# Issuing two 64-row merge products of a block inverse in turn on two quarters of TensorE

## The chip, the cores and the metric

The kernel runs on one core of a Trainium2 chip. The metric is the device time of one execution in microseconds (us), the median of several runs. The engines are named as the profile names them: PE (TensorE, matrix products), PEld (its weight loads), DVE (VectorE), ACT (ScalarE), POOL (GpSimd) and SP (SyncE, which issues most DMAs).

## The reference

One layer of a small language model over an input of 2 sequences of 2048 tokens with 128 channels. The first half is a gated delta rule with 8 heads of 128 by 128 state; the second half is a mixture of 8 experts with top-2 routing. What matters here is the recurrence of the first half:

```python
def step(S, inp):
    q_t, k_t, v_t, beta_t, alpha_t = inp
    S = S * alpha_t[..., None, None]
    kv = jnp.einsum('bhk,bhkv->bhv', k_t, S)
    S = S + jnp.einsum('bhk,bhv->bhkv', k_t, (v_t - kv) * beta_t[..., None])
    o_t = jnp.einsum('bhk,bhkv->bhv', q_t, S)
    return (S, o_t)
```

Taken over a chunk of 128 tokens, these steps become matrix products, and one of the factors is the inverse of a unit triangular 128 by 128 matrix for each head.

## The kernel before

**Tiling.** The 4096 tokens are 32 chunks of 128, worked on in 16 groups of two chunks (`GC = 2`, chunk 0 and chunk 1 of the group). A round of the program finishes group g (the inverse's merges, the solution, the state update, the output) while it prepares group g + 1 (projections, convolution, the matrix to be inverted, and the inverses of its diagonal blocks on DVE). After the 16 groups comes the mixture of experts, which the change does not touch.

**Order.** Every engine runs its own instructions in the order of one list written out by hand, `ORDER` (lines 248 to 264), read once for each round. An entry names a step and its arguments; each engine issues its part of a step where the entry stands, so an entry's place sets the order of each engine's queue, and semaphores tie the engines together. In the last round nothing is prepared.

**The inverse.** DVE inverts the 32 by 32 diagonal blocks (step `inv`, lines 1029 to 1062). They go out to memory and come back (steps `to`, `tp`, `ti`, `tj`) into the tile `T64` (printed as `T` in the profile), and DVE transposes them into `R` (step `rdiag.0` for blocks 1 and 3, `rdiag.1` for blocks 0 and 2, line 1187). Then, for each chunk c, four steps `m.c.hop` on PE with a copy `me.c.hop` on ACT behind each build the rest of the inverse (function `merge`, lines 1460 to 1501):

- hop 0 and hop 1 make the off-diagonal 32 by 32 blocks. Their products stand on 32-row and 32-column parts of PE, two or three streams in turn (lines 1469 and 1470, then 1480 to 1482).
- hop 2 is the last but one product: `Nm[0:64]` against `T64[0:64]`, 8 heads, one 64 by 64 product each, from partitions 0 to 63 to partitions 64 to 127 (line 1490). It waits for `r32_sb` (the copy behind hop 1, lines 808 to 810).
- hop 3 is the last product: `Y64[64:128]` against `R[64:128]`, 8 heads, from partitions 64 to 127 to partitions 0 to 63 (line 1500). It waits for `rdiag.1` and for `y64_sb` (the copy behind hop 2, line 813). The copy behind it, line 817, sets `R_ready`, which the step `u` waits for (line 1602).

A 32-bit product is recorded as two passes, so 8 heads give 16 instructions. Chunk 0's hops 0 and 2 write the bank `ob0` and hops 1 and 3 write `ob1`; chunk 1's write `kx0` and `kx1`. Each hop begins with one or two `carry` products (line 1386), small 16-bit products on all rows whose result is overwritten.

**The steps around it.** `proj` is a projection (lines 1551 to 1553); `taps`, `first`, `last` are the convolution behind it on ACT (766), DVE (1144, 1147) and POOL (639). `kk` forms key products (line 1539, released to DVE's `nm`, line 1163), `ks` the key-state product (1597, then `rhs` on ACT, 822), `u` the solution (1606), `sp` scales the state on POOL (651), `scan` is a decay scan on DVE (1155). The matrices that `nm` makes are written to memory (`no`) and read back (`bi`) before DVE can start the next inverse (line 1042).

The stretch of the order in question runs: `m.1.2 ... proj.6 rdiag.1 me.1.2 m.0.2 ... proj.7 ... kk.0.0 ... m.1.3 ks.0.1 taps.7 me.0.2 proj.8 rhs.0.0 first.7 proj.9 ... me.1.3 m.0.3 ... kk.0.1 ... kk.1.0 u.0.0`.

Of the kernel before, what the change touches and what calls it, by code (L numbers as in the profile page):

```python
# [6 lines left out]
def preln_delta_moe_kernel(nc, x_in, qkv_t, z_t, ab_t, conv_w, dt_bias, a_log, norm_w, out_t,  # L7
# [6 lines left out]
    H = ab_t.shape[1] // 2  # L14
# [31 lines left out]
    with ctx:  # L46
# [18 lines left out]
        wab_lo = sb("wab_lo", [128, 2 * H], F16)  # L65
# [5 lines left out]
        taps = sb("taps", [128, NT, TAPS])  # L71
# [20 lines left out]
        Nm, AT = part(1, 0), part(1, 1)  # L92
        kd = part(2, 0)
        squares, spare = part(2, 1)[:, 0], part(2, 1)[:, 1]
        R, zg = part(3, 0), part(3, 1)
# [5 lines left out]
        T64 = sb("T64", [128, GC, H, 2 * BLK])  # L101
# [7 lines left out]
        rhs = sb("rhs", [128, H, C])  # L109
# [57 lines left out]
        merge_banks = [ob, kx]  # L167
# [58 lines left out]
        def rsqrt_step(s, v, y, t):  # L226
# [21 lines left out]
        ORDER = """  # L248
            v.0.0 diag.0 proj.0 proj.1 v.0.1 taps.0 first.0 proj.2 taps.1 first.1 rdiag.0 proj.3 taps.2 m.1.0 first.2 taps.3
            m.0.0 al.0 proj.4 me.1.0 aq.0 me.0.0 m.1.1 first.3 scan.0 m.0.1 last.0 al.1 xl.0 taps.4 last.1 me.1.1 first.4  # L250
            ka.0 proj.5 last.2 ac.0 ks.0.0 m.1.2 diag.1 taps.5 first.5 me.0.1 proj.6 rdiag.1 me.1.2 m.0.2 last.3 taps.6
            proj.7 last.4 kk.0.0 first.6 m.1.3 ks.0.1 taps.7 me.0.2 proj.8 rhs.0.0 first.7 proj.9 last.5 last.6 me.1.3 m.0.3
            nm.0.0 rhs.0.1 last.7 taps.8 sp.0 kk.0.1 scan.1 nm.0.1 first.8 last.8 me.0.3 kk.1.0 u.0.0 taps.9 kk.1.1 ue.0.0
            sm proj.10 taps.10 sd.0.0 u.0.1 ue.0.1 nm.1.0 nm.1.1 first.9 st.0.0 proj.11 taps.11 last.9 o.0.0 first.10 sq.0.0
            first.11 sd.0.1 ka.1 proj.12 proj.13 no.0 no.1 bi last.10 taps.12 last.11 ktr.0.0 taps.13 o.0.1 st.0.1 g.0.0
            v.1.0 scale.0 first.12 first.13 sq.0.1 ks.1.0 proj.14 kd.0.0 inv.0 rhs.1.0 aq.1 sp.1 proj.15 v.1.1 ks.1.1
            taps.14 taps.15 kq.0.0 inv.1 inv.2 u.1.0 rhs.1.1 u.1.1 g.0.1 inv.3 inv.4 inv.5 first.14 last.12 ue.1.0 ue.1.1
            inv.6 o.1.0 s2 o.1.1 inv.7 at.0.0 inv.8 inv.9 sd.1.0 sq.1.0 inv.10 inv.11 sq.1.1 ac.1 ktr.0.1 first.15 last.13
            inv.12 kd.0.1 last.14 ktr.1.0 last.15 rms.0 scale.1 kd.1.0 sd.1.1 rms.1 gn.0.0 kq.0.1 inv.13 gt.0.0 at.0.1
# [11 lines left out]
        def chunks(b, c):  # L271

            return (b + 1) * GC + c + 1

        def rounds(b):

            return b + 2
# [1103 lines left out]
        def _(pe):  # L1381
            mm, tr = nc.tensor.matmul, nc.tensor.transpose

            def carry(o, w=wab_hi):

                mm(o, w[:, :], w[:, :], start=True, stop=True)
# [44 lines left out]
            def bank_free(use, g, a, r=None):  # L1431

                uses = BANK_USES[bank_of(*use)]
                k = uses.index(use)
                waited = False
                for back in range(1, len(uses) + 1):
                    step, *arg = uses[k - back]
                    early, late = step in PREPARES, step in ROUTES
                    if k >= back:
                        b = a if early else r if late else None if isinstance(g, int) and g == NG else g  # L1440
                        sure = True
                    elif g is None:
                        return
                    elif late:
                        b = None if r is None or isinstance(r, int) and r == 0 else r - 1
                        sure = isinstance(r, int)
                    else:
                        b = g if early else g - 1
                        sure = early or isinstance(g, int) and g > 0
                    if b is None or waited and not early and not late:  # L1450
                        continue
                    if early and isinstance(b, int) and b >= NG:
                        continue
                    for taken, n in released(step, b, *arg):
                        pe.wait_ge(taken, n)
                    if sure:
                        return
                    waited = waited or not late

            def merge(g, a, r, c, hop):  # L1460

                y_bank, r_bank = merge_banks[c]
                if hop == 0:
                    pe.wait_ge(t_in, g * (16 * NB) + 16 * NB)
                    bank_free(("m", c, 0), g, a, r)
                    carry(y_bank[0:2 * H, 0:2 * H])
                    py = y_bank[:, 0:H * BLK].rearrange("p (h c) -> p h c", h=H)
                    for h in range(H):
                        mm(py[32:64, h], Nm[0:32, c, h, 32:64], T64[0:32, c, h, 0:32], start=True, stop=True)
                        ins = mm(py[96:128, h], Nm[64:96, c, h, 96:128], T32[64:96, c, h, :], start=True, stop=True)  # L1470
                    ins.then_inc(y32_mm[c], 1)
                elif hop == 1:
                    pe.wait_ge(rdiag, chunks(g, 0))
                    bank_free(("m", c, 1), g, a, r)
                    carry(r_bank[96:96 + 2 * H, 0:2 * H])
                    pe.wait_ge(y32_sb[c], rounds(g))
                    carry(r_bank[96:96 + 2 * H, 0:2 * H], wab_lo)
                    pr = r_bank[:, 0:H * BLK].rearrange("p (h c) -> p h c", h=H)
                    for h in range(H):
                        mm(pr[0:32, h], Y32[c][32:64, h, :], R[32:64, c, h, 32:64], start=True, stop=True)  # L1480
                        mm(pr[32:64, h], R[32:64, c, h, 32:64], Y32[c][32:64, h, :], start=True, stop=True)
                        ins = mm(pr[64:96, h], Y32[c][96:128, h, :], R[96:128, c, h, 96:128], start=True, stop=True)
                    ins.then_inc(r32_mm[c], 1)
                elif hop == 2:
                    pe.wait_ge(r32_sb[c], rounds(g))
                    bank_free(("m", c, 2), g, a, r)
                    carry(y_bank[0:2 * H, 0:2 * H])
                    py = y_bank[64:128, :].rearrange("p (h c) -> p h c", h=H)
                    for h in range(H):
                        ins = mm(py[:, h], Nm[0:64, c, h, 64:128], T64[0:64, c, h, :], start=True, stop=True)  # L1490
                    ins.then_inc(y64_mm[c], 1)
                else:
                    pe.wait_ge(rdiag, chunks(g, 1))
                    bank_free(("m", c, 3), g, a, r)
                    carry(r_bank[96:96 + 2 * H, 0:2 * H])
                    pe.wait_ge(y64_sb[c], rounds(g))
                    carry(r_bank[96:96 + 2 * H, 0:2 * H], wab_lo)
                    pr = r_bank[0:64, :].rearrange("p (h c) -> p h c", h=H)
                    for h in range(H):
                        ins = mm(pr[:, h], Y64[c][64:128, h, :], R[64:128, c, h, 64:128], start=True, stop=True)  # L1500
                    ins.then_inc(r64_mm[c], 1)

            def route(step, r, g, a):

# [22 lines left out]
            def stages(g, a, par):  # L1527
# [48 lines left out]
                def finish(step, arg):  # L1576

                    if step == "m":
                        merge(g, a, r, *arg)
                    elif step == "v":  # L1580

                        c, u = arg
# [186 lines left out]
```

## Time and profile before

| | us |
|---|---|
| median of 3 runs (lowest, highest) | 1470.88 (1468.65, 1473.63) |
| the profiled execution's own time | 1456.88 |
| its span, first to last instruction | 1454.8 |
| PE busy in it | 1207.4 |
| DVE busy in it | 1158.9 |
| ACT busy in it | 823.5 |
| POOL busy in it | 728.8 |

The profiled execution is 14.0 us shorter than the median of the runs; 2.1 us of its time lie outside the span. Matrix products on PE overlap, so the distance between the starts of two of them, not the length of one, says how fast PE gets through them. PE's granted clock has two levels in this trace, 2.4 GHz (shown as 1.00) and 1.2 GHz (0.50); its mean is 0.923.

### The profile page before, as it was taken

How to read it: one execution, taken by the hardware profiler on the slowest of the kernel's cores; microseconds unless marked ns; L12 is line 12 of the kernel's file. 1: busy time of each engine (PE TensorE's matmuls, PEld its weight loads, DVE VectorE, ACT ScalarE, POOL GpSimd, SP SyncE). 2: the span in 40 equal slices, each digit the busy share in tenths (PEclk: the TensorE clock that was granted, in tenths of full speed). 3: DMA queues.
4: the chain of work that ended last, by engine and by line, in shares of the span. 5: the costliest groups of instructions: out<-in, count | busy, mean ns of one | idle time of the engine just before them, and what ended most of it. 6: DMA issues, size and time to landing. Idle time of an engine off the chain costs nothing.

```text
span 1454.8 us, 33709 instructions
## 1 busy us (share of the span) xinstructions
PE 1207.4 (83%) x11978; PEld 985.3 (68%) x11978; DVE 1158.9 (80%) x2567; ACT 823.5 (57%) x2497; POOL 728.8 (50%) x601
## 2 busy tenths in 40 slices
PE   0356999999898989898989898989999896389980
PEld 0234868787787878786878686868777775267760
DVE  6878888888888788979788888888888853677774
ACT  1243666566656656575657666666565654255552
POOL 3143645546373737373737465555646341154544
PEclk9986989899999989999989998999999898699996
DMA  6031221213131303131222221221212152322214
GB/s 199 4 91 30 68 66 37 74 37 76 36 82 36 86 27 91 31 92 30 81 42 69 43 68 45 66 74 38 74 37 76 35 147 69 98 61 65 65 46 173
DMA packets 163174, 97.07 MB, mean 67 GB/s; under 512 B 115623, under 2 KB 148269, under 8 KB 161988
## 3 DMA queue, kind: packets, MB, share of 16 engines
q1 hardware_dynamic: 124932, 82.25, 20.8%
q10 hardware_dynamic: 33536, 4.20, 2.0%
q0 software_dynamic: 4544, 8.47, 1.8%
q8 instruction: 100, 1.64, 0.5%
q14 instruction: 62, 0.51, 0.1%
HBM read 73.31 MB, written 24.61 MB: 67 GB/s over the span
## 4 chain that ended last, share of the span: by engine, by line
PE 57%; DVE 15%; ACT 10%; issue 7%; DMA 6%; POOL 2%; SPq 1%; POOLq 1%; ACTq 0%; DVEq 0%
PE kx L1539 7%; PE ob L1640 4%; PE rc L1597 4%; PE rc L1606 4%; PE ob L1625 4%; PE ob L1626 4%; PE rc L1588 3%; PE rc L1589 3%; PE rc L1590 3%; DMA rows_out<-rhs,e_dst 3%; PE rc L1614 2%; DVE blkT L1061 2%; PE pj L1551 2%; ACT area L775 2%; DVE Y_sb L1057 2%
## 5 line engine op out<-in xcount | busy, mean ns | idle before, releaser
L639 POOL TENSOR_TENSOR kq<-tapA,area 128x256 f32<-128x256 f32 x256 | 198.7, 785 | 290.0 <-DVE area L1147 289.0
L1057 DVE TENSOR_TENSOR Y_sb<-blkT,blkN 128x4 f32<-128x4 f32 (+18 forms) x304 | 163.5, 538 | 10.4
L766 ACT ACTIVATE area<-pj,taps 128x256 f32<-128x256 f32 x256 | 120.7, 471 | 86.4 <-PE pj L1553 83.6
L1144 DVE SCALAR_TENSOR_TENSOR tapA<-pj,taps,tapA 128x256 f32<-128x256 f32 x256 | 122.2, 477 | 58.6 <-ACT tapA L766 57.1
L622 POOL TENSOR_TENSOR kq<-kq,area 128x1024 f32<-128x1024 f32 x64 | 152.4, 2382 | 0.0
L611 POOL DMA_INDIRECT rows_in<-rowbuf,dest x64 | 66.2, 1035 | 171.5 <-DVE dest L1133 146.2
L1061 DVE TENSOR_REDUCE blkT<-Y_sb 128x2 f32<-128x4 f32 (+18 forms) x304 | 142.2, 468 | 4.7
L1539 PE MATMUL kx<-kq 128*128 128x128 f32 x1024 | 138.4, 285 | 9.1 <-ACT GTs L849 5.1
L1539 PEld LDWEIGHTS kx<-kq 128*128 128x128 f32 x1024 | 126.1, 197 | 17.5 <-issue 11.1
L668 POOL DMA_INDIRECT rows_out<-rhs,e_dst x78 | 79.7, 1022 | 88.9 <-DVE e_dst L1326 47.9
L1147 DVE SCALAR_TENSOR_TENSOR area<-pj,taps,area 128x256 f32<-128x256 f32 x256 | 121.4, 474 | 0.0
L766 ACT ACTIVATE tapA<-pj,taps 128x256 f32<-128x256 f32 x256 | 120.8, 472 | 0.0
L631 POOL TENSOR_TENSOR decay<-ident,beta 128x1024 f32<-128x1024 f32 x32 | 88.8, 2776 | 43.3 <-DVE w_lo L1013 35.0
L651 POOL TENSOR_TENSOR S<-S,a_end 128x1024 f32<-128x1024 f32 x32 | 93.0, 2906 | 17.1 <-PE ob L1626 17.0
L1625 PE MATMUL ob<-S,kq 128*128 128x128 f32 x512 | 100.1, 277 | 0.0
L1626 PE MATMUL ob<-Us,area 128*128 128x128 f32 x512 | 99.0, 275 | 0.0
L1588 PE MATMUL rc<-w_hi,xn_hi 128*128 128x512 f16 x256 | 97.8, 382 | 0.0
L1589 PE MATMUL rc<-w_lo,xn_hi 128*128 128x512 f16 x256 | 97.8, 382 | 0.0
L1590 PE MATMUL rc<-w_hi,xn_lo 128*128 128x512 f16 x256 | 97.6, 381 | 0.0
L835 ACT ACTIVATE area<-ob 128x128 f32<-128x128 f32 x256 | 67.2, 277 | 42.8 <-PE ob L1626 42.8
L1633 PE MATMUL kx<-ident,Gs 128*128 128x128 f32 x256 | 44.0, 312 | 50.5 <-ACT Gs L844 28.3
L1551 PE MATMUL pj<-xn_hi,w_hi 128*128 128x259 f16 x256 | 73.2, 286 | 14.8 <-DVE area L1147 8.0
(306 smaller groups left out, 3631.0 us busy)
## 6 DMA issues: line engine op xcount, KB each, us to landing
area<-scr_alpha SPq DMA_DIRECT2D x32, 512.0 KB, 4.3
area<-scr_acum SPq DMA_DIRECT2D x32, 512.0 KB, 4.2
blkN<-scr_n SPq DMA_DIRECT2D x32, 256.0 KB, 3.9
area<-rows_in SPq DMA_DIRECT2D x39, 130.0 KB, 2.3
scr_n<-area SPq DMA_DIRECT2D x128, 32.0 KB, 1.6
area<-rows_out SPq DMA_DIRECT2D x4, 1024.0 KB, 8.1
rows_in<-rows_in SPq DMA_DIRECT2D x8, 260.0 KB, 3.6
kq<-in_x SPq DMA_DIRECT2D x4, 512.0 KB, 6.0
```

Of the source, the lines that this page charges most:

```text
L622: nc.gpsimd.tensor_tensor(t, t, acum_b[:, c, :, :], ALU.mult).then_inc(done, 1)
L639: nc.gpsimd.tensor_tensor(dst[:, n % H, :], tapA[:, n % RING, :], tapB[:, n % RING, :], ALU.add).then_inc(conv_done, 1)
L766: ins = nc.scalar.activation(dst[:, n % RING, :], pj[n % 2][:, k:k + GT], ACT.Copy, scale=taps[:, t, k:k + 1])
L1057: ins = nc.vector.tensor_tensor(p4, bc(blkT[:, r0:, j:].rearrange("p r (o m) -> p r o m", o=1), [128, nr, w, wd]), bc(blkN[:, j:j + w, j:] ...
L1061: ins = nc.vector.tensor_reduce(blkT[:, r0:, j:j + w], p4, AX.X, ALU.add, negate=True)
L1144: nc.vector.scalar_tensor_tensor(out=tapA[:, n % RING, :], in0=pj[n % 2][:, 0:GT], scalar=taps[:, order[n], 0:1], in1=tapA[:, n % RING, :] ...
L1539: ins = mm(o, lhs[:, hh, cs], rhs_[:, hh, cs], start=True, stop=True)
L1588: mm(rc[u][:, :], hi, wv_hi[:, k, w], start=(k == 0), stop=False)
L1589: mm(rc[u][:, :], hi, wv_lo[:, k, w], start=False, stop=False)
L1590: mm(rc[u][:, :], lo, wv_hi[:, k, w], start=False, stop=False)
L1625: mm(o, qT[1 - par][:, hh, C * c:C * c + C], S[:, c, hh, :], start=True, stop=False)
L1626: ins = mm(o, AT[:, c, hh, :], Us[:, hh, :], start=False, stop=True)
```

## The change

The last product of chunk 1 (hop 3) is no longer issued where the order has it. It is issued with chunk 0's hop 2: when the step `m.0.2` comes, PE takes the waits and the carries of both, and then issues for each head first the product of hop 2 of chunk 0 and then that of hop 3 of chunk 1. The one reads partitions 0 to 63 and writes 64 to 127 of `ob0`; the other reads partitions 64 to 127 and writes 0 to 63 of `kx1`. The entry `m.1.3` moves up in the order to stand right behind `m.0.2` and issues nothing itself. The other three hop-2 and hop-3 products are issued alone as before. The copies `me.0.2` and `me.1.3` on ACT keep their places. The number of products and carries is the same.

```diff
@@ -248,12 +248,12 @@
...
-            ka.0 proj.5 last.2 ac.0 ks.0.0 m.1.2 diag.1 taps.5 first.5 me.0.1 proj.6 rdiag.1 me.1.2 m.0.2 last.3 taps.6
-            proj.7 last.4 kk.0.0 first.6 m.1.3 ks.0.1 taps.7 me.0.2 proj.8 rhs.0.0 first.7 proj.9 last.5 last.6 me.1.3 m.0.3
...
+            ka.0 proj.5 last.2 ac.0 ks.0.0 m.1.2 diag.1 taps.5 first.5 me.0.1 proj.6 rdiag.1 me.1.2 m.0.2 m.1.3 last.3
+            taps.6 proj.7 last.4 kk.0.0 first.6 ks.0.1 taps.7 me.0.2 proj.8 rhs.0.0 first.7 proj.9 last.5 last.6 me.1.3
...
@@ -1481,24 +1481,32 @@
                         mm(pr[32:64, h], R[32:64, c, h, 32:64], Y32[c][32:64, h, :], start=True, stop=True)
                         ins = mm(pr[64:96, h], Y32[c][96:128, h, :], R[96:128, c, h, 96:128], start=True, stop=True)
                     ins.then_inc(r32_mm[c], 1)
-                elif hop == 2:
-                    pe.wait_ge(r32_sb[c], rounds(g))
-                    bank_free(("m", c, 2), g, a, r)
-                    carry(y_bank[0:2 * H, 0:2 * H])
-                    py = y_bank[64:128, :].rearrange("p (h c) -> p h c", h=H)
+                else:
+                    lower = c if hop == 2 else None
+                    upper = c if hop == 3 else 1 if c == 0 else None
+                    if lower is not None:
+                        pe.wait_ge(r32_sb[lower], rounds(g))
+                        bank_free(("m", lower, 2), g, a, r)
+                        yb = merge_banks[lower][0]
+                        carry(yb[0:2 * H, 0:2 * H])
+                        py = yb[64:128, :].rearrange("p (h c) -> p h c", h=H)
+                    if upper is not None:
+                        pe.wait_ge(rdiag, chunks(g, 1))
+                        bank_free(("m", upper, 3), g, a, r)
+                        rb_ = merge_banks[upper][1]
+                        carry(rb_[96:96 + 2 * H, 0:2 * H])
+                        pe.wait_ge(y64_sb[upper], rounds(g))
+                        carry(rb_[96:96 + 2 * H, 0:2 * H], wab_lo)
+                        pr = rb_[0:64, :].rearrange("p (h c) -> p h c", h=H)
                     for h in range(H):
-                        ins = mm(py[:, h], Nm[0:64, c, h, 64:128], T64[0:64, c, h, :], start=True, stop=True)
-                    ins.then_inc(y64_mm[c], 1)
-                else:
-                    pe.wait_ge(rdiag, chunks(g, 1))
-                    bank_free(("m", c, 3), g, a, r)
-                    carry(r_bank[96:96 + 2 * H, 0:2 * H])
-                    pe.wait_ge(y64_sb[c], rounds(g))
-                    carry(r_bank[96:96 + 2 * H, 0:2 * H], wab_lo)
-                    pr = r_bank[0:64, :].rearrange("p (h c) -> p h c", h=H)
-                    for h in range(H):
-                        ins = mm(pr[:, h], Y64[c][64:128, h, :], R[64:128, c, h, 64:128], start=True, stop=True)
-                    ins.then_inc(r64_mm[c], 1)
+                        if lower is not None:
+                            down = mm(py[:, h], Nm[0:64, lower, h, 64:128], T64[0:64, lower, h, :], start=True, stop=True)
+                        if upper is not None:
+                            over = mm(pr[:, h], Y64[upper][64:128, h, :], R[64:128, upper, h, 64:128], start=True, stop=True)
+                    if lower is not None:
+                        down.then_inc(y64_mm[lower], 1)
+                    if upper is not None:
+                        over.then_inc(r64_mm[upper], 1)
 
             def route(step, r, g, a):
 
@@ -1576,7 +1584,8 @@
                 def finish(step, arg):
 
                     if step == "m":
-                        merge(g, a, r, *arg)
+                        if arg != [1, 3]:
+                            merge(g, a, r, *arg)
                     elif step == "v":
 
                         c, u = arg
```

The third changed line of the order, left out above, differs only by where the lines break.

## Rows read from the trace of the kernel before

**Rows 1.** The profile's page: the chain that ended last, by engine

```profile
PE 57%; DVE 15%; ACT 10%; issue 7%; DMA 6%; POOL 2%; SPq 1%; POOLq 1%; ACTq 0%; DVEq 0%
```

**Rows 2.** The chain of waits, 628 to 641 us: start us, us, what

```profile
629.65 0.38 ACT area L810
...
630.25 1.07 PE ob L1490 x16
...
632.79 1.07 PE kx L1500 x16
...
640.62 0.70 DVE area L1163
```

**Rows 3.** Timeline of PE, eighth round: start us, us, engine, line, what xcount [idle before]

```profile
627.24 1.06 PE L1597 MATMUL rc<-S,kq 128*128 128x128 f32 x8
...
630.18 1.14 PE L1490 MATMUL ob<-T,area 64*64 64x64 f32 x16
...
631.60 1.05 PE L1539 MATMUL kx<-kq 128*128 128x128 f32 x8
632.59 0.18 PE L1386 MATMUL kx<-wab_hi 128*16 128x16 f16 x1
...
632.72 1.14 PE L1500 MATMUL kx<-area 64*64 64x64 f32 x16
633.79 1.16 PE L1597 MATMUL rc<-S,kq 128*128 128x128 f32 x8
...
638.64 1.06 PE L1606 MATMUL rc<-rhs,area 128*128 128x128 f32 x8
```

**Rows 4.** Timeline of ACT, same round

```profile
629.65 0.37 ACT L810 ACTIVATE area<-ob 32x256 f32<-32x256 f32 x1
...
632.66 0.59 ACT L813 ACTIVATE Y_sb<-ob 64x512 f32<-64x512 f32 x1
...
634.98 0.60 ACT L822 ACTIVATE rhs<-rc 128x512 f32<-128x512 f32 x1 [0.50 <-PE rc L1597]
...
636.86 0.59 ACT L817 ACTIVATE area<-ob 64x512 f32<-64x512 f32 x1 [0.55 <-PE ob L1500]
```

**Rows 5.** Timeline of DVE, same round

```profile
629.68 1.41 DVE L1187 STREAM_TRANSPOSE area<-T 32x512 f32<-32x512 f32 x2
...
634.06 2.44 DVE L1155 TENSOR_TENSOR_SCAN decay<-area,decay 128x1024 f32<-128x1024 f32 x1
637.95 0.69 DVE L1163 TENSOR_TENSOR area<-kx,decay 128x512 f32<-128x512 f32 x1 [1.44 <-PE kx L1539]
```

**Rows 6.** Timeline of PE, ninth round

```profile
696.59 1.92 PE L1597 MATMUL rc<-S,kq 128*128 128x128 f32 x8
...
700.30 1.14 PE L1490 MATMUL ob<-T,area 64*64 64x64 f32 x16
```

**Rows 7.** Timeline of ACT, ninth round

```profile
699.86 0.59 ACT L813 ACTIVATE area<-kx 64x512 f32<-64x512 f32 x1 [0.96 <-PE kx L1490]
```

**Rows 8.** Line L813: what ended ACT's idle time before it (us, times)

```profile
  PE kx L1490: 7.0, 7
```

**Rows 9.** Timeline of PE, 32-row products of the eighth round, first and last of 30

```profile
623.35 0.19 PE L1469 MATMUL kx<-T,area 32*32 32x32 f32 x1
...
623.80 0.19 PE L1469 MATMUL kx<-T,area 32*32 32x32 f32 x1
```

**Rows 10.** Stretches: us, busy of PE, PEld, DVE, ACT, POOL, PEclk, DMA share, GB/s

```profile
692.10:695.40 3.30, 3.22 (x145) 2.67 (x147) 3.27 (x6) 3.20 (x10) 3.30 (x2) 1.00 0.22 66
695.50:698.80 3.30, 3.30 (x47) 2.86 (x38) 2.91 (x6) 3.20 (x9) 3.30 (x2) 0.50 0.32 109
736.50:739.80 3.30, 1.23 (x8) 0.84 (x8) 3.23 (x5) 3.30 (x13) 1.76 (x3) 1.00 0.00 0
739.90:743.20 3.30, 2.40 (x9) 1.82 (x10) 3.23 (x7) 1.62 (x5) 0.00 (x0) 0.50 0.00 0
```

**Rows 11.** Line L1042: what ended DVE's idle time before it (us, times)

```profile
  DMA blkN<-scr_n: 16.3, 12
```

More of the change, by code:

```diff
@@ L250, in preln_delta_moe_kernel @@
             m.0.0 al.0 proj.4 me.1.0 aq.0 me.0.0 m.1.1 first.3 scan.0 m.0.1 last.0 al.1 xl.0 taps.4 last.1 me.1.1 first.4
-            ka.0 proj.5 last.2 ac.0 ks.0.0 m.1.2 diag.1 taps.5 first.5 me.0.1 proj.6 rdiag.1 me.1.2 m.0.2 last.3 taps.6
-            proj.7 last.4 kk.0.0 first.6 m.1.3 ks.0.1 taps.7 me.0.2 proj.8 rhs.0.0 first.7 proj.9 last.5 last.6 me.1.3 m.0.3
[L253 to L256, printed above, removed]
+            ka.0 proj.5 last.2 ac.0 ks.0.0 m.1.2 diag.1 taps.5 first.5 me.0.1 proj.6 rdiag.1 me.1.2 m.0.2 m.1.3 last.3
+            taps.6 proj.7 last.4 kk.0.0 first.6 ks.0.1 taps.7 me.0.2 proj.8 rhs.0.0 first.7 proj.9 last.5 last.6 me.1.3
+            m.0.3 nm.0.0 rhs.0.1 last.7 taps.8 sp.0 kk.0.1 scan.1 nm.0.1 first.8 last.8 me.0.3 kk.1.0 u.0.0 taps.9 kk.1.1
+            ue.0.0 sm proj.10 taps.10 sd.0.0 u.0.1 ue.0.1 nm.1.0 nm.1.1 first.9 st.0.0 proj.11 taps.11 last.9 o.0.0 first.10
+            sq.0.0 first.11 sd.0.1 ka.1 proj.12 proj.13 no.0 no.1 bi last.10 taps.12 last.11 ktr.0.0 taps.13 o.0.1 st.0.1
+            g.0.0 v.1.0 scale.0 first.12 first.13 sq.0.1 ks.1.0 proj.14 kd.0.0 inv.0 rhs.1.0 aq.1 sp.1 proj.15 v.1.1 ks.1.1
             taps.14 taps.15 kq.0.0 inv.1 inv.2 u.1.0 rhs.1.1 u.1.1 g.0.1 inv.3 inv.4 inv.5 first.14 last.12 ue.1.0 ue.1.1
```

## The prediction

> **What bounds the kernel now.** I read the chain on the page first, because the change touches only the order of work on one engine: PE holds 57% of it, DVE 15%, ACT 10% [rows 1]. Then the chain piece by piece in one round, the eighth. It comes from ACT's copy behind hop 1 of chunk 0, enters PE with hop 2 of chunk 0, and stays on PE through `proj.7`, `kk.0.0`, hop 3 of chunk 1, `ks.0.1` and hop 3 of chunk 0 until DVE's `nm` at 640.62, which feeds the write and read of the matrices to be inverted [rows 2]. So from `m.0.2` to `nm`, some 10 us of each round, every tenth of a microsecond less on PE counts, and every one more. Third, the timelines of PE, ACT and DVE in that stretch, for what is late where: PE has no gap there, ACT and DVE wait for it [rows 3 to 5]. Fourth, the same places of the ninth round, which looks different: there PE comes late, and ACT waits 0.96 us for hop 2 of chunk 1 before it can copy it [rows 6, 7]. That wait is found 7 times in the trace [rows 8]: so there are two kinds of round, 7 where PE is late (the last, which prepares nothing, among them) and 9 where it is early.
>
> **Removed.** Hop 3 of chunk 1 no longer has PE to itself. In the eighth round `kk.0.0` starts at 631.60; its 8 passes take 0.89 us of the stream (the chain's measure of such a block; 1.05 us with its tail), to 632.49. Then two carries and 16 passes stand before `ks.0.1` at 633.79 [rows 3]. That is 633.79 - 632.49 = 1.30 us, of which 1.07 are products.
>
> **Added beside hop 2.** The 16 passes now alternate with hop 2's on the opposite quarter. The trace has no two 64-row products on two quarters, so I bound it. From below 0: the passes fit wholly in between. From above 1.07 us: they do not overlap at all, and the product costs what it costs alone. The nearest row is the 32-row pair of hop 0, whose two streams stand on different rows and columns of PE too: 15 passes of each line lie between 623.35 and 623.80, so one pass of both takes 0.45 / 14 = 0.032 us [rows 9], about half of the 0.067 us of a single 64-row pass (1.07 / 16) [rows 2]. A pass of half the size takes half the time although two streams run, which is what overlap looks like. I take 0.03 us, the one pass that sticks out at the end, and keep 1.07 as the upper end. The Trainium skill, TensorEngine Tiling (Array Packing), Key Properties, says that tiles operate independently, and its table of speedups allows up to 2x for 64-row and 64-column products; by it the sum would be the same 0.03. No row of before shows it for 64 rows. The Trainium skill, TensorE: Matmul & The Clock Gate, What overlaps and what doesn't, says that a weight load overlaps a running product only when their row groups differ, by which pairing would also free the loads. The trace does not bear that out, since single-stream 64-row passes already follow each other every 0.067 us; I add no gain for it.
>
> **Added: a wait.** Hop 3 of chunk 1 needs `rdiag.1` and the copy of hop 2 of chunk 1. PE now meets these waits at `m.0.2`, ahead of hop 2 of chunk 0, and everything behind it stands in PE's queue: `proj.7`, `kk.0.0`, `ks.0.1`.
> - Early rounds (9). DVE's transposes begin at 629.68 and last 1.41, to 631.09; hop 2 of chunk 0 began at 630.18 [rows 3, 5]. From ACT's copy, done at 629.65 + 0.37 = 630.02, to the first product behind one carry there are 0.16 us; from the first of two carries to the product 0.13 (632.59 to 632.72), so with two some 0.18 from the end of the wait [rows 3, 4]. The pair starts at 631.09 + 0.18 = 631.27, which is 1.09 us late.
> - Late rounds. The transposes are done; what ends last is ACT's copy, 699.86 + 0.59 = 700.45, against a start at 700.30 [rows 6, 7]. With 0.16 for one carry the pair starts at 700.61, 0.31 us late.
>
> **Who waits for the wait.** `taps.7` on ACT needs `proj.7`, which comes 1.1 us late in early rounds. ACT then does `me.0.2` at about 633.8 instead of 632.66, `rhs.0.0`, `me.1.3`, `rhs.0.1` and `taps.8` back to back, and comes to `me.0.3` at about 637.0 instead of 636.86: its gaps of 0.50 and 0.55 us in that stretch [rows 4] pay for the rest. `u.0.0` at 638.64 [rows 3] needs that copy, so 0.9 us of slack are left. On DVE the scan of 2.44 us at 634.06 moves to about 635.2 and ends at 637.6; `nm` behind it waited 1.44 us for PE until 637.95 [rows 5], so it just fits. POOL's `last.7` and its state scaling move by the same 1.1 us; the scaled state is added to only behind `sd`, after `u` and its copy. I cost these at nothing; if the cover is too thin the round loses what sticks out, up to 0.2 us. SP's queue is untouched: the order's move concerns PE alone. `me.1.3` finds its product earlier than before and does not wait.
>
> **Sum over PE.** Early round: 1.09 + 0.03 - 1.30 = -0.18 us. Late round: 0.31 + 0.03 - 1.30 = -0.96 us. The sixteenth round has no preparation between the two products; I take half a late round, -0.5 (ends 0 and -0.96). Together 9 x -0.18 + 6 x -0.96 - 0.5 = -7.9 us on PE.
>
> **What comes through.** Behind `nm` the matrices go out and back, and DVE waited for their return in 12 rounds, 16.3 us in all [rows 11]; there an earlier `nm` comes straight through. In the others DVE reaches that point late, but its own gaps before it are waits for PE. I take 0.8 of the sum: -6.3 us, between 0 and -7.9.
>
> **The clock.** PE's granted clock falls to 1.2 GHz for short stretches. It fell at 695.5 after a stretch from 692.1 in which PE was 3.22 of 3.30 us busy, nearly all of it with 32-row products, and at 739.9 after a stretch in which it was busy 1.23 of 3.30 us [rows 10]. So both idling and small products come before a fall. A `ks` block takes 1.92 us at the low level and 1.06 at the high one [rows 3, 6]; a stretch of 3.3 us at the low level does the work of 1.65, and costs up to 1.65 us while PE is on the chain. Now the change puts, in 9 rounds, an idle wait of 1.09 us between hop 2 of chunk 1 and the pair, all 64-row work, with little more than one projection beside it. That is thinner work than stands there now. The trace cannot say how many of the 9 would fall; the ends are 0 and 9 x 1.65 = 14.9 us. I take 2, one round in five, because the full-size `ks.0.0` stands just ahead: +3.3 us. The rounds in which the clock fell before may also shift, for which I have no sign.
>
> **Forecast.** -6.3 + 3.3 = -3.0 us on a profiled time of 1456.88, to 1453.9. The median of the runs shown is 14.0 us above the profiled execution, so other executions have more low-clock stretches or longer transfers; I carry the difference over unchanged and say 1467.9 us. A measurement of this kernel can tell about 0.3%, 4.4 us, from no change.
>
> **Rivals.**
> - *The clock takes nothing.* Then -6.3 to -7.9 remain, and if more rounds of other executions are late ones, each turned round brings another -0.78: down to about -11 with four more. About 1463.5 us. For it: the eighth round's `ks.0.0` ends just ahead of the stretch. Chance 0.34.
> - *The wait brings the clock down in most early rounds* (slower). Place: between hop 2 of chunk 1 and the pair. Price: 1.65 us each. From five such rounds on (8.3 us against 7.9) the kernel is slower; with nine it is 14.9 - 6.3 = +8.6, 1479.5 us; with seven, 1476. For it: a stretch of mere 32-row products, PE 98% busy, was followed by a fall [rows 10]. Chance 0.15.
> - *The two products do not overlap.* The change then only moves the product: 1.04 more per round, early ones +0.86, late ones +0.08, in all 9 x 0.86 + 6 x 0.08 + 0.5 = +8.7, 1479.6 us. Against it: the 32-row pair [rows 9]. Chance 0.06.
> - *It is hidden.* ACT's later chain, or the transfers behind `nm`, take back what PE gains: 1470.9 us. Against it: 12 waits for the return [rows 11]. Chance 0.08.
>
> **How the numbers follow.** The forecast case has 0.37, with its own range from -6 to +1, about 1465 to 1472. Slower by over 0.3% (above 1475.3): the second and third rival, 0.21. Faster by over 0.3% (below 1466.5): the first rival, 0.34, and 0.05 of the forecast's case at its low edge, 0.39. Within 0.3%: the rest, 0.40. Cases of both signs share the chance, so the range reaches into both: 1460 leaves out only the strongest form of the first rival, 1477.5 takes in the slower cases up to seven falls and leaves out the others; together under 2 in 10.
>
> **What would show it.** Right: in the timeline of PE, lines of hop 2 of `ob0` and hop 3 of `kx1` alternate, 32 passes within about 1.1 us. In early rounds PE idles before a carry, released by DVE's transpose, 0.9 us on from ACT's copy; late rounds show ACT's copy there. `ks.0.1` starts 3.4 us after the old start of hop 2 in early rounds (3.61 before) and 2.65 in late ones. ACT's gaps before `rhs.0.1` and `me.0.3` vanish in early rounds. Wrong: 32 passes over 2 us; a half-clock stretch that begins within 3 us of the pair in more than two rounds; or `nm` at its old distance although `ks.0.1` is earlier. The number of late rounds may shift; if it does by more than three, the sum is off by over 2.3 us without any of the terms being wrong.

## The result, and the profile after

| | before | after |
|---|---|---|
| median of the comparison's runs, us | 1469.77 (4 runs) | 1446.79 (4 runs, 1444.28 to 1451.38) |
| ratio, 95% interval | | 0.9844 [0.9808, 0.988] |
| profiled execution: time, span, us | 1456.88, 1454.8 | 1448.90, 1446.8 |
| mean granted clock in it | 0.923 | 0.927 |

The kernel became 23 us faster. That is outside the range given, 13 us below its low end, and the forecast of 1467.9 is 21 us off. All ratios here leave out executions more than 1.5% above the fastest one of their kernel, while the medians are of all.

On the page of the changed kernel PE is busy 20 us less than in the table ahead, DVE 3 us less, and in the chain that ended last PE has given six points, eight went to DVE [rows 1].

```profile
PE 1187.3 (82%) x11978; PEld 967.4 (67%) x11978; DVE 1155.6 (80%) x2567; ACT 818.5 (57%) x2497; POOL 728.8 (50%) x601
...
PE 51%; DVE 23%; DMA 8%; issue 7%; ACT 6%; POOL 2%; SPq 2%; POOLq 1%; DVEq 0%; ACTq 0%
```

The changed kernel's lines are numbered anew: hop 2 is L1503, hop 3 L1505, `kk` L1547, `ks` and `u` L1606 and L1615. The timeline of PE in its eighth round, an early one, shows the pair (columns as in [rows 3]):

```profile
622.09 0.18 PE L1386 MATMUL ob<-wab_hi 128*16 128x16 f16 x1
623.02 0.18 PE L1386 MATMUL kx<-wab_hi 128*16 128x16 f16 x1 [0.76 <-DVE area L1187]
623.06 0.17 PE L1386 MATMUL kx<-wab_lo 128*16 128x16 f16 x1
623.15 0.27 PE L1503 MATMUL ob<-T,area 64*64 64x64 f32 x1
623.16 0.27 PE L1505 MATMUL kx<-area 64*64 64x64 f32 x1
...
624.08 0.22 PE L1503 MATMUL ob<-T,area 64*64 64x64 f32 x1
624.09 0.22 PE L1505 MATMUL kx<-area 64*64 64x64 f32 x1
624.24 0.28 PE L1559 MATMUL pj<-xn_hi,w_hi 128*128 128x259 f16 x1
...
627.26 1.14 PE L1505 MATMUL ob<-area,Y_sb 64*64 64x64 f32 x16
```

The 32 passes start within 0.94 us; hop 2's 16, counted by themselves, within 624.08 - 623.15 = 0.93. Each pass of hop 3 starts 0.01 us behind its partner, so the overlap is full. The price is on the second line: PE idles 0.76 us until DVE's transposes are done. Hop 3 of chunk 0 now comes 4.11 us behind hop 2 of chunk 0. DVE's timeline shows both ends, the transposes and the last `nm`, which comes 9.06 us behind hop 2 where it came 10.44 behind it [rows 2, 3]:

```profile
621.56 1.41 DVE L1187 STREAM_TRANSPOSE area<-T 32x512 f32<-32x512 f32 x2
...
632.21 0.69 DVE L1163 TENSOR_TENSOR area<-kx,decay 128x512 f32<-128x512 f32 x1 [0.61 <-PE kx L1547]
```

So far all is as forecast. What was not shows when a whole round is cut at five marks: the first pass of hop 2 of chunk 0, the start of the last `nm`, the start of L1042 behind the matrices' way out and back, the end of the inversion on DVE (the last L1061), and the end of the round's last transpose (L1187). In an early round of the kernel before, hop 2 starts ahead of that end, and the last stretch counts as negative there. Means over the 15 rounds that prepare a next one, in us, worked out from the starts and ends in the traces, for four profiles of the kernel before, three of the changed one and two of a variant that comes below:

| stretch | before (4) | after (3) | one product behind the other (2) |
|---|---|---|---|
| hop 2 to the last `nm` | 10.62 | 9.39 | 10.88 |
| out and back, to L1042 | 9.55 | 9.61 | 9.59 |
| inversion, L1042 to L1061 | 32.64 | 32.09 | 32.08 |
| to the end of the transposes | 16.43 | 16.27 | 16.29 |
| to the next hop 2 (the wait) | 0.23 | 0.98 | 0.80 |
| the round | 69.47 | 68.34 | 69.63 |

A round is 1.13 us shorter, 15 of them 17 us. The merges give 1.23 - 0.75 = 0.48 of it. The inversion gives 0.55, and the change doesn't touch it; the two stretches between give 0.10 together. So the inversion gives a little more than the merges.

The wait by kinds of round: in an early one hop 2 started 0.90 us ahead of the transposes' end and now starts 0.19 behind it, 1.09 us more, as the prediction had it (25 and 20 rounds). In a late one it started 0.37 behind and now starts 0.76 behind, 0.39 more where the prediction had 0.31 (28 and 17 rounds; those with a longer fall of the clock ahead of hop 2 are left out, and so are the first and the last round).

The views of one round at that place (the stretches of [rows 10] continued, columns as there) show what differs. Before, the clock stays at 1.2 GHz for three stretches from 739.9, and DVE runs dry:

```profile
743.30:746.60 3.30, 2.72 (x14) 1.45 (x13) 2.48 (x9) 2.93 (x9) 0.00 (x0) 0.50 0.00 0
746.70:750.00 3.30, 3.30 (x17) 3.30 (x17) 2.21 (x7) 0.00 (x0) 1.17 (x1) 0.50 0.00 0
750.10:753.40 3.30, 2.96 (x26) 2.75 (x25) 3.12 (x6) 1.57 (x3) 2.55 (x3) 1.00 0.27 84
```

After, the same work has one:

```profile
732.60:736.00 3.40, 3.40 (x15) 2.26 (x14) 3.16 (x7) 2.02 (x6) 0.00 (x0) 0.51 0.00 0
736.10:739.40 3.30, 2.46 (x24) 2.06 (x23) 3.09 (x12) 1.68 (x6) 0.00 (x0) 1.00 0.00 0
739.50:742.80 3.30, 2.96 (x27) 2.75 (x25) 3.16 (x7) 1.57 (x3) 2.21 (x3) 1.00 0.15 45
```

DVE is busy 2.48 and 2.21 of 3.30 us at the low clock, and 3.09 and 3.16 where the clock has come back; in the first stretch at the low clock it is still fed, 3.23 and 3.16. What it waits for is PE's output product, ahead of L1212, `xres<-ob,xres`. Before, what ended DVE's idle time at L1212:

```profile
  PE ob L1640: 13.1, 11
```

and after:

```profile
  PE ob L1649: 8.6, 7
```

Stretches of 10.2 us at 1.2 GHz in this place: 19 in the 60 rounds of before's four profiles, 2 in the 45 of after's three. DVE's idle time within the inversion went from 2.79 to 2.31 us a round, which is nearly all that the stretch lost. Of the 0.48, 0.35 stood ahead of L1212 and most of the rest ahead of L1095, which waits for PE too.

### The profile page after: what moved, and what is told of

It reads as the page before. It is cut to its first block, busy times and chain, and to the rows that moved or that the text cites. A ratio compares the mean times of both kernels' runs of the same rounds, so it can differ in the third digit from the quotient of the medians.

```text
span 1446.8 us, 33709 instructions
## 1 busy us (share of the span) xinstructions
PE 1187.3 (82%) x11978; PEld 967.4 (67%) x11978; DVE 1155.6 (80%) x2567; ACT 818.5 (57%) x2497; POOL 728.8 (50%) x601
## 4 chain that ended last, share of the span: by engine, by line
PE 51%; DVE 23%; DMA 8%; issue 7%; ACT 6%; POOL 2%; SPq 2%; POOLq 1%; DVEq 0%; ACTq 0%
PE kx L1547 7%; PE ob L1649 4%; PE rc L1606 4%; PE rc L1615 3%; PE ob L1634 3%; DVE blkT L1061 3%; PE rc L1597 3%; PE rc L1598 3%; PE rc L1599 3%; DMA rows_out<-rhs,e_dst 3%; PE ob L1635 3%; DVE Y_sb L1057 3%; PE rc L1623 2%; PE pj L1559 2%; POOL rows_out L668 2%
## 5 line engine op out<-in xcount | busy, mean ns | idle before, releaser
L1547 PE MATMUL kx<-kq 128*128 128x128 f32 x1024 | 141.1, 288 | 9.1 <-ACT GTs L849 5.1
L1061 DVE TENSOR_REDUCE blkT<-Y_sb 128x2 f32<-128x4 f32 (+18 forms) x304 | 142.2, 468 | 4.7
L1547 PEld LDWEIGHTS kx<-kq 128*128 128x128 f32 x1024 | 129.2, 201 | 17.7 <-issue 11.1
L775 ACT ACTIVATE area<-kx,kd_scale 128x128 f32<-128x128 f32 x256 | 73.1, 376 | 17.8 <-PE kx L1545 16.2
```

What stands on the lines that cost most here:

```text
L1061: ins = nc.vector.tensor_reduce(blkT[:, r0:, j:j + w], p4, AX.X, ALU.add, negate=True)
L1547: ins = mm(o, lhs[:, hh, cs], rhs_[:, hh, cs], start=True, stop=True)
```

## The experiments

Where idle products are added, their results are not used. Times of one kernel spread, for the changed one from 1443.95 to 1455.85 us, for before from 1452.92 to 1494.09 over 106 executions with a mean of 1470.6, the shorter ones at a higher mean granted clock; so each median is told with its number of runs. The kernel before was timed again beside each group. The expectations speak of what was believed when they were written.

**Is the first profile of before a usual execution?** The kernel before, three times with no edit, and the changed kernel twice more.

> The kernel before, unchanged, for a second profile of it. Theory A: the execution profiled first (1456.9 us) was an unusually quick one, and a usual one (1468 to 1474 us) holds more PE time at 1.2 GHz or more rounds in which PE comes late to hop 2 of chunk 0. Then this profile shows about 1468 us and over 130 us at 1.2 GHz between 140 us and the last round, against 119 us in the first profile. Theory B: the clock is the same in both and the transfers of the inverse's blocks (write and read back) take longer; then the 1.2 GHz time stays near 119 us and the distance from the last nm of a round to DVE's line 1042 grows by some 0.8 us a round.

> A further profile of the kernel before, to meet a usual execution (1462 to 1472 us). Theory A: it has more rounds in which PE is late at hop 2 of chunk 0 than the 7 of 16 of the first profile (9 or more), each with a stretch at 1.2 GHz ahead of it and 10 us at 1.2 GHz some 39 us behind it. Theory B: the late rounds are as many, and the longer time lies in the transfers.

> A fourth profile of the kernel before. If long falls (over 7 us at 1.2 GHz, ending behind hop 2 of chunk 0) are what lifts a usual execution over the quickest ones, an execution above 1465 us has one to three of them, and one under 1460 us none.

> The changed kernel once more, for the spread of its executions. The 29 executions of the kernel before lie between 1454.7 and 1480.9 us at a mean granted clock of 0.908 to 0.927, and the longer ones have the lower clock. If the change works through PE's time alone, its executions have before's clock (about 0.918) and lie near 1458 us. If the larger part of its gain is the clock, they have about 0.930 and lie near 1446 us as in the first four.

> The changed kernel, so that it stands on one chip with the next two. Ratio 0.984 to 0.987. In its profile no stretch at 1.2 GHz at the merges lasts over 10.3 us, while the kernel before had one of 17.1 us in two of its four profiles.

Measured: `e1_before` 1470.18 (10 runs), ratio 1.0034 [0.9997, 1.0071] to its twin; its profiled execution was again a short one, 1454.70 at a clock of 0.924. `e6_before_look` took 1478.26 and `e12_before_look` 1471.40, at 0.914 and 0.913. The changed kernel: 1451.76 (6 runs), ratio 0.9862 [0.9811, 0.9914], and 1451.01 (6), 0.9845 [0.9795, 0.9896]. Its mean clock over 12 runs is 0.930, before's over 106 is 0.917. So the first two profiles of before both come from its short edge. The other two differ in two things. They have more late rounds, as the waits at L813 show; in `e12_before_look`:

```profile
  PE kx L1490: 14.6, 12
```

against 7 [rows 8] and 8 in the short ones, and 9 in `e6_before_look`; after has 8, 5 and 14 of them. And the clock can fall long across the merges. In `e6_before_look`, twelfth round, hop 2 of chunk 0 at 909.64 (stretches, columns as in [rows 10]):

```profile
902.80:911.30 8.50, 8.40 (x101) 7.24 (x101) 5.55 (x9) 5.05 (x13) 5.54 (x4) 0.50 0.36 133
911.30:919.80 8.50, 8.50 (x51) 7.09 (x51) 3.91 (x5) 4.05 (x8) 5.29 (x3) 0.50 0.01 2
919.90:923.00 3.10, 3.10 (x35) 3.03 (x34) 1.07 (x3) 1.31 (x3) 0.00 (x0) 1.00 0.00 0
```

That is 17.1 us at 1.2 GHz with PE busy throughout; the last `nm` comes at 924.61, 14.97 us behind hop 2. In the 15 rounds that prepare a next one, such a fall is in five places of the traces, all of kernels with hop 3 by itself behind `kk.0.0`; with hop 3 at hop 2's place, in one loop or two, no fall there lasts over 10.2 us. In the last round, which prepares nothing, both kinds have falls of up to 20.5 us.

**The overlap or the place?** The same order and waits, but hop 3 behind hop 2 and not in turn, on two chips.

```diff
                             down = mm(py[:, h], Nm[0:64, lower, h, 64:128], T64[0:64, lower, h, :], start=True, stop=True)
+                    for h in range(H):
                         if upper is not None:
```

> The changed kernel with the two products at the same place, but all 8 heads of hop 2 first and then all 8 of hop 3. Theory A (the gain is the overlap of the two quarters): the pair takes 2 x 1.07 us instead of 1.09, 16 rounds x 1.0 = +16 us against the changed kernel, about 1463 us. Rival (the gain comes from moving hop 3 up and leaving one switch between product sizes): under 3 us of difference, 1447 to 1450 us.

> The two products one after the other at the pair's place, beside the changed kernel on one chip. By time on the chain at the rate of the dense products of e7 (18.5 us for 0.75 us a round, 1.5 us for each) it is 18 us above the changed kernel. If thin work costs more than dense work of the same length, it is 24 us or more above it.

Measured: 1471.27 (10 runs), 1.0037 [1.0003, 1.0071]; 1473.93 (12 runs), 1.0014 [0.9978, 1.0049]. The whole gain is gone, so the overlap is needed for it. PE's timeline of `e17_one_then_other2`, eighth round, hop 2 L1503 and hop 3 L1506:

```profile
635.42 0.97 PE L1503 MATMUL ob<-T,area 64*64 64x64 f32 x13
636.18 0.27 PE L1506 MATMUL kx<-area 64*64 64x64 f32 x1
...
636.40 0.92 PE L1506 MATMUL kx<-area 64*64 64x64 f32 x13
637.25 0.29 PE L1560 MATMUL pj<-xn_hi,w_hi 128*128 128x259 f16 x1
```

Hop 3 starts 0.76 us behind hop 2, so at full clock the overlap is worth some 0.75 us a round, 11 us in 15; the projection behind comes 1.83 us behind hop 2 instead of 1.09. Measured are 22.9 us on one chip (1473.93 against 1451.01). The last column of the table says where most of the rest is. A round is 1.29 us longer there than in the changed kernel, 19 us in 15: hop 2 to `nm` is 10.88 against 9.39, 1.49 and not 0.75, while all other stretches are within 0.18 of after's. The difference goes with the clock. At full clock `nm` comes at 9.79 in this variant and at 9.05 in the changed kernel. Above that lie 1.09 us a round in the variant, 0.34 in the changed kernel, and above 10.44 in before 0.18. In the variant's 30 rounds the clock falls at the pair (from 0.5 us ahead of it to 1 us behind) 9 times, 7 of them for 6.8 us; in the changed kernel's 45 rounds 6 times, each for 3.4. One of the former, in `e17_one_then_other2`, hop 2 at 283.1:

```profile
283.40:286.70 3.30, 3.30 (x34) 3.05 (x32) 0.83 (x2) 0.00 (x0) 1.57 (x3) 0.50 0.45 153
286.80:290.10 3.30, 3.30 (x17) 3.27 (x17) 2.27 (x4) 2.50 (x5) 1.31 (x2) 0.50 0.00 0
```

And the inversion is as short in this variant, 32.08, as in the changed kernel: that gain does not need the overlap. It goes with the place of hop 3 here, though not in every order that has it there (`e3_proj_first` below lacks it). Moving alone costs 0.26 + 0.57 us a round at the merges and wins 0.56 in the inversion, so that the round is 0.16 longer; overlapping wins 1.29.

**What is a microsecond on PE worth here?** Seven full-size products, 0.75 us, ahead of each pair (dense work, where the variant above adds thin work), and three of them ahead of each hop 1 of the kernel before:

```diff
+                    if lower == 0 and upper == 1:
+                        for _ in range(7):
+                            mm(yb[:, 0:256], w_hi[:, 0:128], w_hi[:, 0:256], start=True, stop=True)
```

```diff
                     carry(r_bank[96:96 + 2 * H, 0:2 * H], wab_lo)
+                    for _ in range(3):
+                        mm(r_bank[:, 0:256], w_hi[:, 0:128], w_hi[:, 0:256], start=True, stop=True)
```

> The changed kernel with 7 full-size 16-bit products of 256 columns (0.75 us in all) in front of each pair, overwritten by the pair. Their time on PE is what issuing the two products one after the other costs (nm 0.75 us later in each round in that run's profile), but PE is full in it. If that run's +24 us over the changed kernel were PE time alone, this one gives the same, 1469 to 1471 us. If half of it was the clock falling over thin work at the pair, this one costs only the 16 x 0.75 = 12 us, 1457 to 1460 us, and no stretch at 1.2 GHz begins within 1 us of a pair.

> The kernel before with 3 full-size products of 256 columns (0.32 us) in front of each hop 1, 0.64 us a round, overwritten by it. Theory A (the falls behind the 32-row products are what makes rounds late, and a large part of before's spread): no stretch at 1.2 GHz ends within 5 us before hop 2 of chunk 0, the granted clock rises to 0.93, and in spite of 10 us more work the time is at most before's (1458 to 1466 us). Rival: the clock there costs little, and the time is 1474 to 1478 us.

Measured: the first 1470.31 (12 runs), 0.9987 [0.995, 1.0023], that is 18.6 us above the changed kernel on the same chip for 12 us of work. In its profile a round is 69.21 us, 0.87 above after's mean, nearly all in the last stretch (1.92 for 0.98), and hop 2 to `nm` stays at 9.20. So dense work costs about its own time in the rounds. No fall begins at the pair (from 0.5 us ahead of it to 1 us behind), where the thin variant has 9 in 30 rounds; two of 3.4 us begin 1.5 and 1.8 us ahead of it, and this is one profile. The rest of its 18.6 us is not placed, and as times, 18.6 for the dense work and 22.9 for the thin are not told apart. The second, 1471.11 (12 runs), 0.996 [0.9913, 1.0007]: 0.64 us more PE work in a round, and the kernel isn't slower. Its profiled execution was a long one, 1476.75, but not by the rounds: they take 68.97 us each where before's take 69.47, and what follows hop 2 of the last round takes 293 us where before's four profiles have 269 to 281. The clock fell near the merges in one round of 15 (for 17.1 us), where before has 6 to 11, and the inversion takes 32.16 for 32.64. DVE's idle time at L1212 ended by PE:

```profile
  PE ob L1642: 6.0, 4
```

An edit that only adds work ahead of the merges shortens the same stretch, 40 us on, that the change shortens. Over the 17 profiles of both kernels and their variants without the 32-row products, the time at 1.2 GHz within the inversion is 3.0 to 6.6 us a round, and the stretch lasts 32.0 to 32.75 in step with it (correlation 0.93, 0.20 us for each us at the low level). Before has 6.0 on average, after 3.6.

**Density alone?** Idle 64-row products on the opposite quarter, beside hop 2 of chunk 0 of the kernel before, and beside the two single products of the changed one:

```diff
                         ins = mm(py[:, h], Nm[0:64, c, h, 64:128], T64[0:64, c, h, :], start=True, stop=True)
+                        if c == 0 and h < H - 1:
+                            side = merge_banks[1][1][0:64, :].rearrange("p (h c) -> p h c", h=H)
+                            mm(side[:, h], ow[64:128, h, 0:64], ow[64:128, h, 64:128], start=True, stop=True)
```

> The kernel before with 7 idle 64-row products (results overwritten) in turn with hop 2 of chunk 0 on the opposite quarter, as hop 3 stands there in the changed kernel; the true hop 3 stays where it was. Nothing leaves PE's chain. If the changed kernel gains beyond its 0.3 to 1.1 us a round because PE's work at hop 2 of chunk 0 is denser and the clock comes back sooner, this one keeps that part: granted clock above before's 0.916, ratio 0.988 to 0.993, long falls (over 7 us) at the merges rarer. If the gain needs the shorter way through PE (less time at thin work, an earlier kk), it is as before: ratio 0.998 to 1.002.

> The changed kernel with such idle products also beside the two single 64-row products that are left (hop 2 of chunk 1, hop 3 of chunk 0). If density decides, the stretches at 1.2 GHz that begin at the pair (3 of 16 rounds in one profile, 1 in the other) go, the clock rises above 0.930, and it is 2 to 6 us under the changed kernel, ratio 0.981 to 0.984. If not, the same ratio as the changed kernel, 0.984 to 0.986.

Measured: before 1464.76 (12 runs), 1.0009 [0.9974, 1.0044]; after 1441.60 (6), 0.9827 [0.9779, 0.9875]. Two streams in one place, with nothing moved, change nothing: inversion 32.61. The ratio of the second is not told apart from the changed kernel's 0.9845; the changed kernel itself was not timed on that chip.

**The new wait.** `proj.7` ahead of the pair, and the transposes earlier on DVE:

```diff
-            ka.0 proj.5 last.2 ac.0 ks.0.0 m.1.2 diag.1 taps.5 first.5 me.0.1 proj.6 rdiag.1 me.1.2 m.0.2 m.1.3 last.3
-            taps.6 proj.7 last.4 kk.0.0 first.6 ks.0.1 taps.7 me.0.2 proj.8 rhs.0.0 first.7 proj.9 last.5 last.6 me.1.3
+            ka.0 proj.5 last.2 ac.0 ks.0.0 m.1.2 diag.1 taps.5 first.5 me.0.1 proj.6 rdiag.1 me.1.2 last.3 proj.7 m.0.2 m.1.3
+            taps.6 last.4 kk.0.0 first.6 ks.0.1 taps.7 me.0.2 proj.8 rhs.0.0 first.7 proj.9 last.5 last.6 me.1.3
```

```diff
-            ka.0 proj.5 last.2 ac.0 ks.0.0 m.1.2 diag.1 taps.5 first.5 me.0.1 proj.6 rdiag.1 me.1.2 m.0.2 m.1.3 last.3
+            ka.0 proj.5 last.2 ac.0 ks.0.0 m.1.2 diag.1 taps.5 rdiag.1 first.5 me.0.1 proj.6 me.1.2 m.0.2 m.1.3 last.3
```

> The changed kernel with proj.7 ahead of m.0.2 in the order, so that a projection (0.33 us) runs in the wait before the pair. Theory A (PE is on the chain there and the wait costs its length): in early rounds 0.33 us less each, some 9 rounds, -3 us, and fewer stretches at 1.2 GHz that begin at the pair (3 in the profile after), each worth up to 1.7 us: 1438 to 1444 us. Rival (ACT or DVE is the bound there by now): no change, 1446 us.

> The changed kernel with DVE's rdiag.1 ahead of first.5 instead of behind it. The transposes end 0.8 us earlier, so the pair waits for ACT's copies instead (0.45 us behind the start of before in early rounds, not 0.90), but first.5 and with it proj.7 come up to 1.4 us later. Theory A (the transposes are what the pair waits for): 0.4 us less in early rounds, -4 us, about 1443 us. Rival (first.5 is then late and proj.7 waits for it): no gain or up to +0.5 us a round, 1447 to 1455 us.

> proj.7 ahead of the pair and the idle 64-row products, beside the changed kernel on one chip. Before: 0.982 on one chip against 0.986 and 0.984 on others. If the wait filled by proj.7 counts, it is 3 to 7 us under the changed kernel; if that was the chip, within 2 us.

Measured: 1444.99 (4 runs), 0.9841 [0.9756, 0.9925]; 1447.31 (4), 0.9848 [0.9765, 0.9931]; and the first together with the idle products 1449.62 (6), 0.9861 [0.9806, 0.9916]. None is told apart from the changed kernel. With `proj.7` in the wait `nm` comes 8.80 us behind hop 2 at full clock, 0.25 earlier where 0.33 was hoped for, but the clock spends 5.9 us a round low in the inversion, as before the change, and that stretch is 32.59 again. With early transposes the stretch up to them is 0.7 shorter and the wait behind them 0.8 longer: in every round the pair now starts 0.16 us behind the end of ACT's copy of hop 2 of chunk 1 (L813), which is late next.

**Denser 32-row products, and all together.** Idle 32-row products beside hops 0 and 1 (the first of three places is shown), in the kernel before, in the changed one, and with everything above:

```diff
+                        if h < H - 1:
+                            mm(py[0:32, h], ow[32:64, h, 0:32], ow[32:64, h, 32:64], start=True, stop=True)
...
```

> The kernel before with idle 32-row products (results not used) in turn with the true ones of hops 0 and 1, on rows and columns of PE that stand empty. They should take no time of their own. Theory F (in a usual execution most rounds are late, because the clock falls behind the 32-row products, and each such fall costs 1 to 2 us): falls at the merges go from 8 to 11 a profile to 3 or fewer, and the ratio is 0.985 to 0.991. Rival (late rounds cost little, the chain makes it up elsewhere): falls go, ratio 0.996 to 1.001.

> The changed kernel with the same idle 32-row products. With few late rounds in either kernel the change is worth only its early-round price, 0.3 us (4.5 us in all). Theory F, that the rest of its 22 us is late rounds and the falls with them: this one is then only 4 to 8 us (0.3 to 0.6%) under e13, ratio 0.980 to 0.986, little changed from the changed kernel. Rival (the gain is PE time wherever the clock stands): it keeps its 1.5% against e13, ratio 0.972 to 0.978.

> Both proj.7 ahead of the pair and the idle products beside the single ones. By the wait's price (0.24 us less from PE's view in each early round, some 3 us) and the clock (2 to 6 us) it is the quickest, ratio 0.978 to 0.983. If neither counts, 0.984 to 0.986.

> The idle 32-row products with proj.7 ahead of the pair and the idle 64-row products beside the single ones (ratio 0.982 without the 32-row ones). If falls at the merges (6 in that profile) still cost 1 us or more each, 0.975 to 0.979; if not, 0.981 to 0.983.

Measured: 1499.87 (6 runs), 1.0205 [1.016, 1.025]; 1461.66 (12), 0.996 [0.9936, 0.9985]; `e11_proj_beside`, without the 32-row part, 1440.81 (6), 0.9821 [0.9775, 0.9868]; `e15_best`, with it, 1453.69 (7), 0.9914 [0.9882, 0.9945]. The 32-row products harm both kernels. The falls that they were to remove did not go: the first has 9 near the merges in its 15 rounds, two of them of 17.1 us, the second 5. A hop of four streams takes 0.54 us where two or three took 0.50, but from hop 0 to hop 2 of chunk 0 the profiles are 1.5 and 0.9 us longer than the means of before's four and after's three, which this doesn't cover; it stays open. The change itself is worth more between these two, 38 us, than between the kernels without the idle products. No version here is shown to beat the changed kernel: `e11_proj_beside` and `e18_proj_beside2` are one kernel at 0.9821 and 0.9861, whose intervals overlap with each other and with 0.9845.

## Why the prediction was wrong

**What held.** PE bounds the stretch from hop 2 to `nm`, and hop 3's 1.30 us came off it: 10.44 became 9.05 at full clock, 1.39. The overlap is full, and the third rival falls. The Trainium skill, TensorEngine Tiling (Array Packing), Key Properties, says tiles work independently, and for 64 rows the trace now agrees: 0.94 us for both products, 0.92 for one alone (the 1.14 of L1505 at 627.26, less its last pass of 0.22). The wait is there, behind the transposes in early rounds and behind ACT's copy in late ones, and its size held: the sum had it at (9 x 1.09 + 6 x 0.31) / 15 = 0.78 us a round, and the table has 0.98 - 0.23 = 0.75. The clock's term in its place held too: 3, 1 and 2 falls begin at the pair in three profiles, where two were taken, at 1.55 us each where 1.65 was taken. That the spans of the first two profiles differ by 8.0 and the sum over PE was 7.9 is chance. Between these two the merges lose 15 x (1.06 - 0.93) = 2.0 us, where the prediction's terms make a gain of 4.6: the changed kernel's profile has three falls at the pair, and its wait ahead of the last round is 4.2 us longer. The inversion gives 11.5 us, and all the rest takes 1.5 back.

**What failed, first: "The rounds in which the clock fell before may also shift, for which I have no sign."** It was costed at nothing. Of the sum's terms it was the one most in error: the rounds' time at 1.2 GHz within the inversion fell from 6.0 to 3.6 us, DVE waits less for PE there, and 0.55 us a round, 8 us in all, came of it. This went with the place of hop 3 in the two profiles with one product behind the other, and work added elsewhere (`e8_before_filled`) went with the same. Why a fall at 39 us behind hop 2 ends after 3.4 us in one order and after 10.2 in the other, no run settles.

**Second: "I carry the difference over unchanged."** The 14.0 us between profile and median were taken to belong to any kernel, so that the forecast is the median of before less 3.0 us; after, the profiled execution is 2.1 us above the median. The sentence gave the reason itself, more low-clock stretches, and so should have asked what the change does to them. The first profile was of a short execution, and usual ones hold more of what the change takes away. Late rounds gain more than early ones: 7 of 16 are late in the first profile, 9 and 12 in the two usual ones, and the prediction names the slope (0.78 for each round turned round) but leaves it out of the forecast. And a fall of 17.1 us across the merges, of which the first profile has none, costs 4.5 us more; both usual profiles have one, the changed kernel's 45 rounds none. Averaged over before's four profiles, falls across the merges make 0.18 us a round, 2.7 us in all.

**Also "I take 0.8 of the sum".** The way out and back is 9.55 before and 9.61 after: all but 0.06 us comes through, behind whichever round.

**The sum again**, in us over 15 rounds: `nm` earlier at full clock -20.9 (1.39), more at the pair's falls +2.4, the wait +11.2, the inversion -8.2, the way out and back +0.8, the stretch up to the transposes -2.4 (not explained); together -17. The ratios say -20 to -23. The profiles of before are on average 5 us quicker than its 106 executions, after's three about 2 us slower than its 16, which covers the rest within the spread. What follows hop 2 of the last round, the mixture of experts in the main, takes 269 to 281 us in these seven profiles, 2.8 us more after than before on average, and takes no part in the gain.

**The rivals.** The first, "the clock takes nothing", had the direction and reached to 11 us: it thought of more late rounds, not of a clock that gives back. The second, the wait bringing the clock down, happens in the thin variant (9 falls in 30 rounds), and is rarer in the changed kernel (6 in 45, each of 3.4 us, where 7 of the 9 lasted 6.8). What was argued and not tried: whether the shorter inversion would vanish if the clock fell as before, since nothing here sets the clock by itself. The evidence is that its length follows the time at 1.2 GHz over 17 profiles and that DVE's waits for PE in it shrink by as much.

## What to carry to other kernels

A single profile is one draw. Where medians and profiled time differ by 1%, look at clock and counts in several executions before a term rests on "7 rounds of 16", and never carry the difference over as a constant: it is made of what the change may alter. Products on opposite quarters are worth pairing when both are on the chain: here 0.75 us of thin work a round, issued by itself, cost its own time and, with falls of the clock, as much again. And after an edit, cut the round at marks on every engine: the gain may stand 40 us from the edit.

## What the runs showed of the hardware

- Two 64-row, 64-column 32-bit products on opposite quarters, issued in turn, took 0.94 us for 32 passes, from the first start to the last, where 16 alone take 0.92. Even issued one behind the other they overlap a little (`e17_one_then_other2`): the second begins 0.76 us behind the first, with three passes of each in turn, where a product alone holds PE for 1.07 [rows 2].
- The granted clock stayed at 1.2 GHz for 17.1 us while PE was busy 16.90 of 17.00 us (`e6_before_look`).
- A small addition of work went with a different pattern of the clock's falls, near it and far from it. With 0.64 us of full-size products a round ahead of the two hop 1s, one profile has a fall near the merges in 1 round of 15, where four profiles of before have 6 to 11, and 3.9 us a round at 1.2 GHz in the inversion, 20 us on and more, where they have 6.0. The kernel with 10 us more work was no slower (0.996 [0.9913, 1.0007]).
